# Layer norm and the loads of x in chunks of 4 tiles in place of 8, with the square root's table loaded first: one attention and mixture-of-experts block

## What is computed

```python
xn = (x - mean(x)) / sqrt(var(x) + 1e-5)
qkv = xn @ w_qkv.T                      # 16 heads, two queries and two keys of 8, one value of 16
o = softmax(q1 k1.T * s) v - lam * softmax(q2 k2.T * s) v
attn = rms_norm(o) * (1 - lambda_init) @ w_proj.T + b_proj
logits = xn @ wg                        # 8 experts, the two best, capacity 1024 tokens each
moe = g1 * expert(idx1) + g2 * expert(idx2)   # gelu(t @ w_gate) @ w_down
out = x + attn + moe
```

## Time and profile before

| | us |
|---|---|
| median of 3 runs | 1758.35 |
| lowest and highest run | 1758.08, 1759.79 |
| the profiled execution | 1758.22 |
| its span in the profile | 1756.4 |
| PE busy | 1704.4 (97%) |
| DVE busy | 1472.2 (84%) |
| ACT busy | 1396.9 (80%) |
| POOL busy | 560.3 (32%) |

### The profile page before, as it was taken

How to read it: one execution, slowest core, us unless ns; L and a number is a source line. 1 busy time by engine, 2 the same in 40 slices (tenths; PEclk the granted TensorE clock), 3 DMA queues, 4 the chain that set the end, 5 groups by cost and what they waited for, 6 DMA issues and landing times.

```text
span 1756.4 us, 39364 instructions
## 1 busy us (share of the span) xinstructions
PE 1704.4 (97%) x15554; PEld 750.7 (43%) x15555; DVE 1472.2 (84%) x1728; ACT 1396.9 (80%) x2637; POOL 560.3 (32%) x1096
## 2 busy tenths in 40 slices
PE   6999999999999999999999999999999999999999
PEld 5558888888884222222222222222222222222237
DVE  7877777777777999999999999999999999999923
ACT  4464534544546999999999999999999999999993
POOL 1124122212100243332433334335543334433353
PEclk9989999999999999999999999999999999999999
DMA  8754333321203111111111111111111111100003
GB/s 261 223 190 134 105 106 102 111 79 47 85 25 114 34 30 41 30 37 35 30 42 30 36 32 33 42 30 33 39 29 40 32 36 37 29 25 11 14 8 103
DMA packets 92280, 109.66 MB, mean 62 GB/s; under 512 B 17472, under 2 KB 67264, under 8 KB 92096
## 3 DMA queue, kind: packets, MB, share of 16 engines
q1 hardware_dynamic: 85952, 90.36, 16.5%
q0 software_dynamic: 6144, 16.79, 3.3%
HBM read 72.77 MB, written 33.82 MB: 61 GB/s over the span
## 4 chain that ended last, share of the span: by engine, by line
PE 67%; ACT 28%; DVE 3%; DMA 1%; issue 1%; ACTq 0%; SPq 0%; DVEq 0%
ACT arena_t L832 25%; PE banks L1287 19%; PE banks L1275 12%; PE banks L1330 10%; PE banks L1308 10%; PE banks L1257 8%; PE banks L1353 2%; ACT o_raw L815 2%; PE banks L1160 2%; PE banks L1388 2%; DVE rest L930 1%; PE banks L1203 1%; PE banks L1192 1%; DMA k_stack<-arena_q 1%; DVE arena_q L937 1%
## 5 line engine op out<-in xcount | busy, mean ns | idle before, releaser
L1045 DVE TENSOR_REDUCE row_half<-banks 128x2 f32<-128x1024 f32 x1024 | 1185.1, 1216 | 117.2 <-PE banks L1257 115.7
L832 ACT ACTIVATE arena_t<-banks 128x512 f32<-128x512 f32 x2048 | 1082.4, 599 | 43.2 <-PE banks L1275 17.5
L1287 PE MATMUL banks<-arena_t,v_ring 128*17 128x256 f32 x8192 | 642.3, 386 | 25.5 <-ACT o_raw L815 25.4
L1287 PEld LDWEIGHTS banks<-arena_t,v_ring 128*17 128x17 f32 x8192 | 136.1, 95 | 408.0 <-issue 240.9
L1275 PE MATMUL banks<-arena_q 50*128 50x512 bf16 x960 | 284.0, 383 | 0.0
L1257 PE MATMUL banks<-arena_q 48*128 48x512 bf16 x960 | 268.0, 383 | 0.0
L1275 PE MATMUL banks<-qk_ring 50*128 50x512 bf16 x896 | 264.0, 385 | 2.7 <-DVE arena_r L1095 2.5
L1257 PE MATMUL banks<-qk_ring 48*128 48x512 bf16 x896 | 248.6, 382 | 1.4 <-DVE rows_parts L989 1.4
L797 ACT ACTIVATE arena_t<-banks 128x512 f32<-128x512 f32 x128 | 76.6, 599 | 201.6 <-PE banks L1308 190.9
L1330 PE MATMUL banks<-w_parts,hidden_parts 128*128 128x256 f32 x1536 | 196.2, 286 | 0.0
L1330 PEld LDWEIGHTS banks<-w_parts,hidden_parts 128*128 128x128 f32 x1536 | 187.0, 191 | 13.7 <-issue 13.6
(11 more groups left out here) (145 smaller groups left out, 1326.8 us busy)
## 6 DMA issues: line engine op xcount, KB each, us to landing
expert_rows<-arena_r SPq DMA_DIRECT2D x16, 512.0 KB, 3.2
q_stack<-arena_q SPq DMA_DIRECT2D x8, 768.0 KB, 3.7
k_stack<-arena_q SPq DMA_DIRECT2D x8, 768.0 KB, 4.1
v_ring<-v_heads SPq DMA_DIRECT2D x64, 68.0 KB, 2.8
arena_x<-x_in SPq DMA_DIRECT2D x4, 1024.0 KB, 6.4
token_rows<-arena_x SPq DMA_DIRECT2D x4, 1024.0 KB, 5.4
arena_v<-w_gate_in SPq DMA_DIRECT2D x4, 1024.0 KB, 6.6
arena_v<-w_down_in SPq DMA_DIRECT2D x4, 1024.0 KB, 8.8
```

The costliest lines, as they stand in the source:

```text
L832: nc.scalar.activation(probs[:, kt % PSLOTS, q, :], banks[:, ST_BANKS[ring_place(i) % 3], :], ACT.Exp).then_inc(exp_done, 1)
L1045: nc.vector.tensor_reduce(halves[:, :, j // 2], banks[:, smax_bank(m):smax_bank(m) + 2, :], AX.X, ALU.max, negate=True).then_inc(smax_done, 1)
L1287: mm = pe.matmul(banks[QUAD * q:QUAD * q + VP, OT_BANK, columns], v_ring[:, g % SLOTS, kt, :], probs[:, kt % PSLOTS, q, columns], start=(k ...
```

## The change

`LN_CHUNK` is 4 in place of 8, so that x comes in eight loads of 512 KB in place of four of 1 MB, and statistics, square root, reciprocal and normalization work on four tiles at a time. `x_in` has eight semaphores. ACT runs one square root on a column of `ident` as soon as that constant is there, which loads the function's table. `load_table` moves up in the code; its later callers pass through the same function, which now reads `ident` in place of `expert_m8`.

```diff
-        x_in = [sem(f"x_in{i}") for i in range(4)]
+        x_in = [sem(f"x_in{i}") for i in range(NT // 4)]
...
-        LN_CHUNK = 8
+        LN_CHUNK = 4
...
         def _(act):
 
+            def load_table(function):
+                nc.scalar.activation(unused[:], ident[:, 0:1], function)
+
             def deviation(i):
...
+            act.wait_ge(consts, 6)
+            load_table(ACT.Sqrt)
             act.wait_ge(consts, 9)
             deviation(0)
...
-            def load_table(function):
-                nc.scalar.activation(unused[:], expert_m8[:, 0:1], function)
-
```

## The result

| | us |
|---|---|
| before, median of 20 runs | 1759.32 (1758.08 to 1761.00) |
| changed, median of 20 runs | 1761.49 (1759.93 to 1763.41) |
| ratio | 1.0014, 95% interval 1.0008 to 1.0020 |
| profiled execution of the changed kernel | 1761.00, span 1759.2 |

The change costs 2.2 us by the medians (1.4 to 3.5 by the interval), 2.8 by the two spans. That is under the 0.2% that was set as the bound of "no change", and its sign is clear. The forecast was +2.6 us.

What follows compares the result with a forecast made beforehand. Matmuls bound the long phases; the change acts only in the first 60 us, where DVE's backlog sets the end. DVE's later release +4.0, CAST stall +0.7, PE's lead -2.1 give +2.6: 1760.9 us, range 1757.8 to 1763.4.

Steps and rivals of the forecast that it cites:

- The sum: Whole kernel: +4.0 for DVE's later routing end, +0.7 for a stalled CAST, -2.1 for PE's lead, giving +2.6 us.
- Start: Loading and normalizing x: first half chunk lands at 5.8, PE's first matmul comes at 11.65, 4.6 us earlier.
- The half rate: PE's early work: half rate for its first 3.6 us, from 15.06 to 18.66, costing v(0) 0.9 us.
- The choice between 0.6, 2.1 and 3.9: PE's lead at the end of v of quad 0: 2.1 us taken, with bounds of 0.6 and 3.9.
- The bound of 0.6: PE's lead if all of v(0) runs at half rate and x lands a little later: 0.6 us.
- The last square root: ACT's list: it moves from quad 4 to quad 6, near 39.4; first routing group near 42.0.
- The cast: DVE's routing under GpSimd's IOTAs: group 1's CAST stalls, +0.7 us; group 2's is free.
- The rival of two stalled casts: Routing: late landing of the last token rows makes IOTAs stall two CASTs; +4.0, 1762.3 us, chance 0.12.
- Its threshold: Last token rows landing over 5.6 us after issue: IOTAs end after 56.98 and catch group 2's CAST too.
- The table load: ACT's early square root table load: 1.28 us, hidden behind DVE's work on chunk 1; costs and gains nothing.
- chunk 0 is through at 7.7: DVE's statistics of the first four tiles end at 7.7 us, so the table load would fit before 9.9.
- Handed on in full: q/k stage and after: DVE is busy 10.00 of 10 us, so the whole +2.6 us shift reaches the end.

Runs made afterwards that it cites:

- experiment 6: Changed kernel with 56 added identity transposes ahead of TensorE's first wait; 1760.48 us, ratio 1.0005 to the kernel before.
- experiment 9: Changed kernel with 56 added transposes ahead of TensorE's first wait and 16 more behind quad 0's; 1759.59 us, ratio 1.0004 to the kernel before.
- experiment 1: Changed kernel with ScalarE's square roots one quad further ahead in its list; 1757.98 us, ratio 0.9996 to the kernel before.
- experiment 4: Changed kernel without the early table load; 1761.69 us, ratio 1.0014 to the kernel before.
- experiment 5: Changed kernel with square roots one quad ahead and sixteen small IOTAs in place of four; 1757.86 us, ratio 0.9990 to the kernel before.
- experiment 2: Kernel before, chunks of 8, with only its last square root moved one quad later; 1761.80 us, ratio 1.0015 to the kernel before.
- experiment 3: Kernel before with the early table load and the rest of the change, but chunks of 8; 1759.36 us, ratio 1.0001.
- experiment 8: Changed kernel with square roots one quad ahead, sixteen IOTAs and 56 added transposes before TensorE's first wait; 1755.70 us, ratio 0.9977.

## Why the prediction was right, point by point

- **The sum.** Forecast +4.0 + 0.7 - 2.1 = +2.6. The profile shows a last group 3.33 later: with 1.95 for PE's lead and a stall of 1.26 (1.49 less 0.23), +4.0 comes out again (3.33 + 1.95 - 1.26 = 4.02). The total moved by +2.8 between the spans and +2.2 between the medians. That it lies so near +2.6 is partly luck: at the end of the stage the forecast was short by 0.7 (0.56 of the stall and 0.15 of the lead), and behind it some 0.5 of the shift was lost, where the prediction had it handed on in full.
- **Start.** x landed at 5.36, 0.4 before the forecast 5.8, and PE's first matmul came at 11.43 (forecast 11.65), the second eight at 14.76 (15.06), the end of v of quad 0 at 21.46 (21.32). The 0.3 us gained at the transposes were lost again at the half rate. Bytes moved until landing, plus the 1.15 us behind the last byte, sized the smaller transfer to 0.4 us.
- **The half rate.** The choice between 0.6, 2.1 and 3.9 was the largest uncertainty. Experiments 6 and 9 show that it is the clock, and that a pause between the two eights matters. The 2.1 is less sure than one profile makes it look: the changed kernel and experiments 1, 4 and 5 have the same list for PE, and v of quad 0 took 4.94, 5.21, 5.46 and 4.48 us in them and ended at 21.46, 21.36, 22.01 and 20.72, a lead of 1.4 to 2.7. The bound of 0.6 was summed wrongly: all of v(0) at half rate is 7.12 us from 16.86, which ends at 23.98, so d would be -0.6 and the time 1763.6, outside the range.
- **The last square root.** Forecast 39.4 and a first group at 42.0; measured 39.57 and 42.14. Experiments 1 and 2 show cause and size in both directions at q's first store: one quad in the place of the square roots in ACT's list is worth 3.4 us in the changed kernel (66.21 - 62.85), and of the last one alone 2.1 in the kernel before.
- **The cast.** The term was mis-sized: 0.7 forecast, 1.26 measured. The store of the last rows took 5.6 us to land, where 5.0 was taken, so the second IOTA ended at 51.05. The rival of two stalled casts comes true where the IOTAs outlast the next cast's start, 55.62; they ended at 54.98, 0.64 before it. Its threshold, a landing over 5.6 us, was worked out wrongly: it held the first stall at 0.7, but that stall grows with the landing and pushes the next cast back by as much, so the 0.64 stays as long as the first cast falls under the second IOTA. It did, 0.57 after that began (49.66, 49.09); a second stall needed a landing of over about 6.2, an estimate from these rows. Experiment 1 shows the other case, a first cast under the first IOTA and the next under the fourth. Experiment 5 agrees with what the Trainium skill (SBUF — State Buffer, "Who interferes with whom") describes, a lock held for one whole instruction: the stall ends with the IOTA under way, and shrinks with its length. That it is a port that is locked, no run here can show.
- **The table load.** Its cost of zero stands (experiments 3 and 4), but the cover was thinner than stated. The prediction let the first square root start at 7.7; it started at 9.11, since the addition of eps in front of it took 1.80 us. The step that failed is "chunk 0 is through at 7.7" for ACT; DVE's later operations hid it.
- **Handed on in full.** Nearly: 3.33 at q's first store, 3.03 at the experts, 2.83 at the end. The 0.3 between q and the experts and the 0.35 in the attention phase are not explained by an experiment. The granted clock fell to 0.50 in the q/k stage of both kernels, from about 98 to 108 us in the kernel before and from about 104 to 111 in the changed one; whether that plays a part, no run tells.

## What to carry to other kernels

Where a chunk size also sets the place of another engine's instruction, look at the last chunk: halving the chunk moved the last square root two quads later, behind work of an engine that had nothing to do with it, and all that DVE had queued behind the normalization became the end of the stage. A faster start is worth only what reaches the stage's last wait, so ask which engine is idle just ahead of that wait, and how much more work it will find queued there. Here 2.2 idle microseconds of DVE were the whole margin.

## What was not expected of the hardware

- DVE's first addition of eps on 128x4 values took 1.80 us in the changed kernel, 0.97 in experiment 4 and between 0.28 and 1.85 in the other profiles with chunks of 4, where the next one took 0.17. It lay under GpSimd's four memsets of 0.9 us each (5.35 to 8.98 in the changed kernel's profile), and in all eight profiles it ended with the end of one of them (near 7.2, 8.1 or 9.0). The cast's behaviour would explain only a part: in experiments 1 and 6 the addition waited for the memset under way, but in the changed kernel and experiment 8 it started just behind the third memset's start (7.21 and 7.16, against 7.14) and ended at 9.01 with the fourth, one later than a cast would. No run took the memsets away.
- The clock column of a window shows 1.00 at the start of every profile read here, also where PE ran at half rate: durations of equal matmuls (1.94 and 1.04 us for eight) tell it, the column doesn't.
- In the changed kernel PE's clock fell after a wait of 3.93 us, and six q/k matmuls took 4.44 us, with no effect on the time, because DVE set the pace.
